# A graph layer on one core: the small fp32 products rewritten as rounded and remainder parts, the left-over rows stacked

## The reference, cut to what matters

```python
h = jnp.maximum(_layernorm(x, axis=-1), 0.0)            # x: 10000 x 128
hi = item_feat @ W_item.T + b_item                      # 10000 x 128
b  = h @ W_user.T + b_user
out = x + relu(adj @ hi + b)                            # adj: 10000 x 10000, f32
```

## Time and profile before

| | |
|---|---|
| median of 3 runs | 1114.21 us (1113.17 to 1114.88) |
| profiled execution, its own time | 1113.8 us |
| its span in the profile | 1112.0 us |
| TensorE busy | 1101.9 us (99%) |
| VectorE busy | 972.7 us (87%) |
| ScalarE busy | 768.1 us (69%) |
| TensorE's granted clock | 1.00 of full speed |
| moved by DMA | 421.50 MB, mean 379 GB/s |

### The profile page before, as it was taken

The page is one execution under the profiler, slowest core; times in us unless marked ns, Lnnn a source line. Parts: engine busy times, 40 slices in busy tenths (PEclk is TensorE's granted clock), DMA queues, the critical chain, the costliest instruction groups (busy, mean ns, idle before and its releaser), DMA issues.

```text
span 1112.0 us, 12241 instructions
## 1 busy us (share of the span) xinstructions
PE 1101.9 (99%) x5026; PEld 904.1 (81%) x5026; DVE 972.7 (87%) x692; ACT 768.1 (69%) x491; POOL 31.0 (3%) x62
## 2 busy tenths in 40 slices
PE   8999999999999999999999999999999999999998
PEld 7788788888888788888887888888788888888887
DVE  6999988889998888899998888999987889888887
ACT  5766766677776667776766677777766767776664
POOL 0000000001000000010000000000000000000000
PEclk9999999999999999999999999999999999999999
DMA  9999999999999999999999999999999999999994
GB/s 358 414 426 393 380 360 364 372 366 380 427 382 378 386 368 389 391 389 425 379 376 386 359 405 388 391 423 375 386 366 379 398 354 401 410 367 352 370 382 165
DMA packets 64904, 421.50 MB, mean 379 GB/s; under 512 B 7999, under 2 KB 8787, under 8 KB 25040
## 3 DMA queue, kind: packets, MB, share of 16 engines
q1 hardware_dynamic: 60128, 406.15, 93.1%
q0 software_dynamic: 4432, 14.44, 3.8%
q10 hardware_dynamic: 288, 0.13, 0.0%
HBM read 415.57 MB, written 5.12 MB: 378 GB/s over the span
## 4 chain that ended last, share of the span: by engine, by line
PE 91%; DVE 5%; DMA 1%; issue 1%; ACT 1%; SPq 0%; DVEq 0%; ACTq 0%
PE acc L578 29%; PE acc L571 29%; PE acc L572 29%; DVE lo_ring L379 4%; PE acc L544 2%; PE acc L521 1%; DMA a_ring<-in_adj_tiles 1%; ACT hi_ring L315 1%; DVE y L459 1%; PE acc L537 1%; PE acc L554 0%; DVE centred L422 0%; DVE stat L418 0%; SPq L219 0%; SPq L237 0%
## 5 line engine op out<-in xcount | busy, mean ns | idle before, releaser
L379 DVE TENSOR_TENSOR lo_ring<-a_ring,hi_ring 128x2048 fp32r<-128x2048 f32 (+1 forms) x387 | 861.5, 2239 | 120.3 <-ACT hi_ring L315 119.9
L315 ACT CAST hi_ring<-a_ring 128x2048 fp32r<-128x2048 f32 (+1 forms) x387 | 725.1, 1874 | 326.4 <-PE acc L578 321.6
L571 PE MATMUL acc<-hi_ring,h_lo 128*128 128x512 f32 (+1 forms) x1560 | 614.0, 394 | 1.2 <-ACT hi_ring L324 0.6
L578 PE MATMUL acc<-lo_ring,h_hi 128*128 128x512 f32 (+1 forms) x1560 | 603.0, 387 | 3.7 <-DVE lo_ring L379 3.7
L572 PE MATMUL acc<-hi_ring,h_hi 128*128 128x512 f32 (+1 forms) x1560 | 599.9, 385 | 0.0
L578 PEld LDWEIGHTS acc<-lo_ring,h_hi 128*128 128x128 f32 x1560 | 292.9, 188 | 68.1 <-DVE lo_ring L379 7.5
L571 PEld LDWEIGHTS acc<-hi_ring,h_lo 128*128 128x128 f32 x1560 | 293.1, 188 | 65.8 <-issue 9.1
L572 PEld LDWEIGHTS acc<-hi_ring,h_hi 128*128 128x128 f32 x1560 | 293.5, 188 | 61.9 <-issue 4.6
L521 PEld LDWEIGHTS acc<-wi,items 128*128 128x128 f32 x156 | 22.0, 196 | 2.0
L273 POOL DMA_DIRECT2D rows<-in_x_rows x20 | 10.9, 546 | 419.9 <-DVE centred L422 375.9
L521 PE MATMUL acc<-wi,items 128*128 128x128 f32 x156 | 22.2, 280 | 0.0
(11 more groups left out here) (31 smaller groups left out, 118.3 us busy)
## 6 DMA issues: line engine op xcount, KB each, us to landing
a_ring<-in_adj_tiles SPq DMA_DIRECT2D x311, 1024.0 KB, 7.1
a_ring<-in_adj_tiles SPq DMA_DIRECT2D x78, 904.0 KB, 6.6
rows<-in_x_rows POOLq DMA_DIRECT2D x19, 256.0 KB, 6.1
y<-in_x_t POOLq DMA_DIRECT2D x19, 256.0 KB, 7.1
items<-in_item_t SPq DMA_DIRECT2D x12, 384.0 KB, 7.7
out_t<-y POOLq DMA_DIRECT2D x16, 256.0 KB, 6.4
a_ring<-in_adj_tiles SPq DMA_DIRECT2D x4, 256.0 KB, 5.2
out_t<-y SPq DMA_DIRECT2D x3, 256.0 KB, 2.5
```

The lines of the kernel that those rows point to most:

```text
L315: nc.scalar.copy(hi_ring[:, r, 0:group_w(g)], a_ring[:, s, 0:group_w(g)]).then_inc(hi_written, 1)
L379: nc.vector.tensor_tensor(lo_ring[:, r, 0:n], a_ring[:, s, 0:n], hi_ring[:, r, 0:n], ALU.subtract).then_inc(lo_written[s], 1)
L571: nc.tensor.matmul(acc[k][:, 0:bank_w(g, k)], h_lo[:, c, :], hi, start=(c == 0), stop=False, skip_group_check=True)
L578: last = nc.tensor.matmul(acc[k][:, 0:bank_w(g, k)], h_hi[:, c, :], lo, start=False, stop=(c == CHUNKS - 1), skip_group_check=True)
```

## The change

The user product becomes three fp32r products: W_user is split once into `wu_hi` and `wu_lo`; ScalarE's copy out of PSUM now writes the rounded part `turned_hi`, and a new VectorE subtraction after tile 18 + 12k writes `turned_lo`. The products come before tile 20 + 12k instead of 18 + 12k.

The left-over product of a bank becomes one fp32r product over 50 rows. The moving side has the 16 adj rows three times (rounded, rounded, remainder) and two rows of ones; the weights are the rounded h, the remainder of h, the rounded h, and the rounded and remainder parts of b_user. Two banks stand side by side, at partitions 0 and 64, and the other two beside them in the free direction. SyncE loads 50 rows of 512 for each bank; at c = 38 ScalarE rounds 50 rows of 1024 twice and VectorE subtracts 16 rows of 1024 twice. `h_rem_product` moves from before tile 36 to before tile 10 of group 0, GpSimd moves six small pieces of the weights from SBUF to SBUF once, and `squares` and `normed` share a buffer. The descriptor scratch of the DMAs that GpSimd issues is set to 8192.

```diff
-ROWS_BLOCK = 32
+PAIR = 2
+ROWS_BLOCK = 64
+REM_ROWS = 3 * REM + 2
+REM_HI = 2 * REM
-H_REM_AT = 3 * BODY
-REM_AT = H_REM_AT + 4
+H_REM_AT = 10
+REM_AT = 3 * BODY + 4
+REM_ROUND_AT = REM_AT - 2
+WU_AT = 12
-USER_AT = 18
+USER_AT = 20
...
-                    sp.wait_ge(rem_used, g)
+                    sp.wait_ge(rem_lo_set, PAIR * g)
                 for k in range(ACC_BANKS):
-                    row = k * ROWS_BLOCK
-                    sp.dma_start(a_rem[row:row + REM, 0:bank_w(g, k)], adj_rem[g * ACC_BANKS + k, :, 0:bank_w(g, k)]).then_inc(rem_loaded, 16)
+                    row, n = k % PAIR * ROWS_BLOCK, BANK_W
+                    sp.dma_start(a_rem[row:row + REM_ROWS, k // PAIR, 0:n], adj_rem[g * ACC_BANKS + k, :, 0:n]).then_inc(rem_loaded, 16)
...
+            def move_rem_weights():
+
+                pool.wait_ge(h_rem_lo_set, 1)
+                pool.wait_ge(user_hi_set, 2)
+                pool.wait_ge(user_lo_set, 2)
+                for part in range(PAIR):
+                    row = part * ROWS_BLOCK
+                    pool.dma_start(h_rem[row + REM:row + 2 * REM, :], h_rem_lo[:, :]).then_inc(rem_moved, 16)
...
+            def left_over_round(g):
+                act.wait_ge(rem_loaded, (g + 1) * (16 * ACC_BANKS))
+                if g > 0:
+
+                    act.wait_ge(rem_used, g)
+                for part in range(PAIR):
+                    rows_p = slice(part * ROWS_BLOCK, part * ROWS_BLOCK + REM_ROWS)
+                    nc.scalar.copy(rem_parts[rows_p, :, :], a_rem[rows_p, :, :]).then_inc(rem_hi_set, 1)
...
-                act.wait_ge(turned_ready, g * UNITS + k + 1)
-                nc.scalar.copy(normed_t[:, 0:bank_w(g, k)], turned_of(g)[:, 0:bank_w(g, k)]).then_inc(normed_t_ready, 1)
+                u, n = g * UNITS + k, bank_w(g, k)
+                act.wait_ge(turned_ready, u + 1)
+                if u > 0:
+
+                    act.wait_ge(user_done, u)
+                nc.scalar.copy(turned_hi[:, 0:n], turned_of(g)[:, 0:n]).then_inc(turned_hi_set, 1)
...
+            def left_over_subtract(g):
+                for part in range(PAIR):
+                    rows_p = slice(part * ROWS_BLOCK + REM_HI, part * ROWS_BLOCK + REM_HI + REM)
+                    dve.wait_ge(rem_hi_set, g * PAIR + part + 1)
+                    nc.vector.tensor_tensor(rem_parts[rows_p, :, :], a_rem[rows_p, :, :], rem_parts[rows_p, :, :],
+                                            ALU.subtract).then_inc(rem_lo_set, 1)
+
+            def turned_subtract(g, k):
+                u, n = g * UNITS + k, bank_w(g, k)
+                dve.wait_ge(turned_hi_set, u + 1)
+                nc.vector.tensor_tensor(turned_lo[:, 0:n], turned_of(g)[:, 0:n], turned_hi[:, 0:n], ALU.subtract).then_inc(turned_lo_set, 1)
...
-                nc.tensor.matmul(acc_of(g)[k][:, 0:bank_w(g, k)], wu[:, :], normed_t[:, 0:bank_w(g, k)], start=False, stop=False,
-                                 skip_group_check=True)
+                nc.tensor.matmul(out[:, 0:n], wu_lo[:, :], turned_hi[:, 0:n], start=False, stop=False, skip_group_check=True)
+                nc.tensor.matmul(out[:, 0:n], wu_hi[:, :], turned_hi[:, 0:n], start=False, stop=False, skip_group_check=True)
+                pe.wait_ge(turned_lo_set, u + 1)
+                nc.tensor.matmul(out[:, 0:n], wu_hi[:, :], turned_lo[:, 0:n], start=False, stop=False,
+                                 skip_group_check=True).then_inc(user_done, 1)
...
-                pe.wait_ge(rem_loaded, (g + 1) * (16 * ACC_BANKS))
+                pe.wait_ge(rem_lo_set, PAIR * (g + 1))
                 for k in range(ACC_BANKS):
-                    rows_k = slice(k * ROWS_BLOCK, k * ROWS_BLOCK + REM + 1)
-                    last = nc.tensor.matmul(acc_of(g)[k][:, 0:bank_w(g, k)], h_rem[rows_k, :], a_rem[rows_k, 0:bank_w(g, k)],
+                    row, n = k % PAIR * ROWS_BLOCK, bank_w(g, k)
+                    rows_k = slice(row, row + REM_ROWS)
+                    last = nc.tensor.matmul(acc_of(g)[k][:, 0:n], h_rem[rows_k, :], rem_parts[rows_k, k // PAIR, 0:n],
                                             start=False, stop=False, skip_group_check=True)
```

More of the change, by code:

```diff
@@ L46 @@
 RING_GAP = 96
+DMA_SCRATCH = 8192
 CHUNKS = N_ITEM // P
@@ L78 @@
 assert PIECES * PIECE_TRIOS == TRIOS and PIECES == LOADS
-assert REM < ROWS_BLOCK and ACC_BANKS * ROWS_BLOCK <= P
+assert REM_ROWS <= ROWS_BLOCK and PAIR * ROWS_BLOCK <= P and ACC_BANKS % PAIR == 0
 F32 = mybir.dt.float32
@@ L170, in graph_layer @@
         rem_loaded = sem("rem_loaded")
-        ones_loaded = sem("ones_loaded")
+        rem_moved = sem("rem_moved")
+        rem_hi_set = sem("rem_hi_set")
+        rem_lo_set = sem("rem_lo_set")
+        h_rem_lo_set = sem("h_rem_lo_set")
+        user_hi_set = sem("user_hi_set")
+        user_lo_set = sem("user_lo_set")
         rows_loaded = sem("rows_loaded")
@@ L245, in _ @@
             sp.dma_start(wu[:, :], w_user_t).then_inc(user_loaded, 16)
[L246 to L249, removed]
+            sp.dma_start(bu[:, :], b_user).then_inc(user_loaded, 16)
             for g in range(GROUPS):
@@ L332, in h_rem_round, with user_round @@
                 act.wait_ge(h_rem_summed, 1)
-                for k in range(ACC_BANKS):
-                    row = k * ROWS_BLOCK
-                    nc.scalar.copy(h_rem[row:row + REM, :], h_full_rem[:, :]).then_inc(rem_set, 1)
+                for part in range(PAIR):
+                    for at in (0, REM_HI):
+                        row = part * ROWS_BLOCK + at
+                        nc.scalar.copy(h_rem[row:row + REM, :], h_full_rem[:, :]).then_inc(rem_set, 1)
+            def user_round():
+                act.wait_ge(user_loaded, 2 * 16)
+                nc.scalar.copy(wu_hi[:, :], wu[:, :]).then_inc(user_hi_set, 1)
+                nc.scalar.copy(bu_hi[:, :], bu[:, :]).then_inc(user_hi_set, 1)
+            def left_over_round(g):
[5 more added lines that the diff above has]
+                    nc.scalar.copy(rem_parts[rows_p, :, :], a_rem[rows_p, :, :]).then_inc(rem_hi_set, 1)
             def square(g, k):
@@ L363, in _ @@
                         h_round_hi(c // TRIO + 1)
-                    if g == 0 and c == REM_AT:
+                    if g == 0 and c == WU_AT:
+                        user_round()
+                    if g == 0 and c == H_REM_AT + 4:
                         h_rem_round()
+                    if c == REM_ROUND_AT:
+                        left_over_round(g)
                     for at, step in ((SQUARE_AT, square), (SQRT_AT, root_of_var), (COPY_AT, copy_turned)):
@@ L406, in h_rem_add_bias, with h_rem_subtract_lo, user_subtract_lo @@
                 nc.vector.tensor_tensor(h_full_rem[:, :], h_rem_bank[0:REM, 0:HID], bi[0:REM, :], ALU.add).then_inc(h_rem_summed, 1)
+            def h_rem_subtract_lo():
+                dve.wait_ge(rem_set, 1)
+                nc.vector.tensor_tensor(h_rem_lo[:, :], h_full_rem[:, :], h_rem[0:REM, :], ALU.subtract).then_inc(h_rem_lo_set, 1)
+            def user_subtract_lo():
+                dve.wait_ge(user_hi_set, 1)
+                nc.vector.tensor_tensor(wu_lo[:, :], wu[:, :], wu_hi[:, :], ALU.subtract).then_inc(user_lo_set, 1)
+                dve.wait_ge(user_hi_set, 2)
+                nc.vector.tensor_tensor(bu_lo[:, :], bu[:, :], bu_hi[:, :], ALU.subtract).then_inc(user_lo_set, 1)
+            def left_over_subtract(g):
+                for part in range(PAIR):
+                    rows_p = slice(part * ROWS_BLOCK + REM_HI, part * ROWS_BLOCK + REM_HI + REM)
[6 more added lines that the diff above has]
+                nc.vector.tensor_tensor(turned_lo[:, 0:n], turned_of(g)[:, 0:n], turned_hi[:, 0:n], ALU.subtract).then_inc(turned_lo_set, 1)
             steps = 6
@@ L494, in _ @@
                         empty(g - 1, 3)
-                    for at, step in ((CENTRE_AT, centre), (VAR_AT, variance), (NORM_AT, norm)):
+                    if c == REM_ROUND_AT:
+                        left_over_subtract(g)
+                    for at, step in ((CENTRE_AT, centre), (VAR_AT, variance), (NORM_AT, norm), (COPY_AT + 1, turned_subtract)):
                         k = unit_at(c, at)
@@ L633 @@
     left[:N_USER] = adj[:, full:]
+    left_rows = np.ones((GROUPS * ACC_BANKS, REM_ROWS, BANK_W), np.float32)
+    for part in range(3):
+        left_rows[:, part * REM:(part + 1) * REM] = left.reshape(GROUPS * ACC_BANKS, BANK_W, REM).transpose(0, 2, 1)
     x_rows = np.zeros((GROUPS * UNITS, ROW_T, ROW_TILES, HID), np.float32)
@@ L640 @@
         "adj_tiles": tiles.reshape(GROUPS, GROUP_W, CHUNKS, P).transpose(0, 2, 3, 1).reshape(GROUPS * CHUNKS, P, GROUP_W),
-        "adj_rem": left.reshape(GROUPS * ACC_BANKS, BANK_W, REM).transpose(0, 2, 1),
-        "ones_row": np.ones((1, BANK_W), np.float32),
+        "adj_rem": left_rows,
         "item_t": np.asarray(L0_gnn_item_feat).T,
```

49 lines of the change are left out of this document (36 added, 13 removed).

## The result

The changed kernel takes 1115.92 us (median of 20 runs, 1114.5 to 1118.16), the kernel before 1114.28 (20 runs). The ratio is 1.0015, with a 95% interval of 1.0008 to 1.0021: slower by 0.15%, less than the 0.2% set as the bound, and clear of zero. The forecast was 1111.8 with a range of 1109.0 to 1114.2; the time lies outside it. The profiled execution has a span of 1114.3 us, 2.3 more than before.

A forecast was written before the change was run, and what follows sets the result against it. TensorE was taken to bound the kernel, driving a ring, if later stages keep up. 3.8 + 2.1 - 2.1 - 0.6 - 0.1 - 0.6 = 2.5 us off 1113.8 gave 1111.3, median 1111.8, range 1109.0 to 1114.2.

The forecast's parts named there:

- User product: TensorE's user product: three fp32r products cost 0.68 us against 0.88 for fp32, saving 0.20 a unit, 3.8 us in all.
- Left-over products: TensorE's left-over products of a group: 0.84 us instead of 1.27, saving 0.43 a group, 2.1 us in five.
- no toll: Rival: the 0.39 us for switching from 128 rows to blocks and back vanishes with fp32r; 1110.2 us, chance 0.14.
- pairs don't run side by side: Rival: TensorE's two pairs of 50-row left-over products run one after another, costing 1.30 us; 1113.5 us, chance 0.15.
- VectorE's left-over subtractions: Two subtractions after tile 38 make TensorE wait 0.5 us at tile 39, 41 in group 0: -2.1 and -0.6 us.
- 1.22 at 1024 and 1.13 back to back; the pair is 2.26: VectorE's 1024-wide left-over subtraction: time in us set by width, alone, in a row, and for two.
- margin of 1.80: Tile 39, group 1: 1.80 us from the end of VectorE's subtraction to bank 0's third product on TensorE.
- no VectorE stall: Rival: the left-over subtractions cost 1.2 us or are taken up, so TensorE does not wait; 1109.1 us, chance 0.08.
- The loads: Four left-over loads ahead of tile 12 grow from 32 to 100 KB: 0.2 to 0.3 us in group 0, -0.6 total.
- Delays of 0.65 to 1.2 us: How much later tiles behind the larger left-over loads land, by bytes at 425 GB/s or by fewer DMA engines.
- the slow rival: 50-row loads make tile 12 3.6 us late, costing 12 us over five groups, 1123 us; chance 0.08 with other slow cases.
- The moved h_rem_product: The product L527, moved before tile 10 of group 0, costs the same there, perhaps 0.1 us more: -0.1.

The follow-up runs named there:

- user part alone: Kernel before with only the user product split into three fp32r products before tile 20 + 12k, left-over part untouched: 1111.23 us, ratio 0.9976.
- casts_early: Changed kernel with ScalarE's two left-over casts after tile 34 instead of 38, VectorE's subtractions still after 38: 1115.79 us, ratio 1.0020.
- rows48: Changed kernel with left-over loads of 48 rows instead of 50, the two rows of ones loaded once at the start: 1116.26 us, ratio 1.0019.
- not in place: Changed kernel with the first left-over subtraction of a group writing to its own tile, not over its input, and descriptor scratch 4096: one profiled run, 1115.98 us.
- late loads: Changed kernel with the four 50-row left-over loads of a group issued ahead of tile 24 instead of tile 12: 1114.13 us, ratio 1.0000.

## Why the prediction was wrong

It had the mechanisms and nearly all their places, and mis-sized three terms, all to the same side: measured 1115.9 against 1111.8. The three are 1.3, 2.5 and 1.2 us off, 5.0 together where the forecast is off by 4.1; two of them are read from medians and one from the ledger of one profile, so they need not add up.

- **User product, 3.8 forecast.** The user part alone gained 2.5 us by the medians (0.24% by the ratio); in its profile 0.9 came from elsewhere. The step that failed is "three fp32r products cost 0.68": in this place they cost 0.72, and some products behind them come 0.235 apart instead of 0.227, so a unit gave 0.13 (0.08 in group 0), not 0.20. That VectorE's new subtraction is hidden was right.
- **Left-over products, 2.1 forecast.** Right: 0.87 against 1.27, 2.0 in five groups, with the toll that the prediction kept. By the rule of the Trainium skill, "TensorEngine Tiling (Array Packing)", section Key Properties (a change of mode drains TensorE), the trace agrees: L647 starts 0.32 us after the product before it, where L554 started 0.31 after, so the late start stands in blocks of 64 rows as of 32, with fp32r as with fp32. That the late start is a drain, the trace alone doesn't show. The rivals "no toll" and "pairs don't run side by side" fall.
- **VectorE's left-over subtractions, -2.1 and -0.6 forecast.** Forecast at half its size, at the right tiles but for one: 0.96 us in group 1 instead of 0.5, 1.0 a group in five, 5.2 us where 2.7 stood. In group 0 the wait was forecast at tile 41 alone and fell on 39 and 41, at 0.5 each. The step that failed is "1.22 at 1024 and 1.13 back to back; the pair is 2.26". The 1.22 was exact (mean 1219 ns). But the overlap of 0.09 with the neighbours, which "back to back" took for granted, is missing at all three seams and a gap of 0.03 stands there, which makes 0.12 a seam, so the pair takes 2.62; and TensorE's restart costs 0.11 more. Since the margin of 1.80 is subtracted from the whole, 0.36 us more of burst and 0.11 of restart doubled the wait. The rival "no VectorE stall" falls; `casts_early` shows that ScalarE's casts were hidden, as argued.
- **The loads, -0.6 forecast.** They cost 1.8 us by the median, 1.9 in group 0 of this profile. The step that failed is "Delays of 0.65 to 1.2 us": tile 12 landed 15.3 us after its issue where it had 12.5, 2.8 later. That is later than the 2.2 from which the slow rival was to decide, and one of the prediction's signs of being wrong (ScalarE's wait for loads grows by several us: 4.3 to 8.5) came true. But the rival's price was wrong too: it had all five groups pay, and in this profile only group 0 did, as the tiles of group 1 came 0.5 to 1.7 later and still in time. The Trainium skill, "DMA: Bandwidth & Descriptors", section Why a DMA increments its semaphore by 16 and not by 1, would have 50 rows on 10 engines and 48 rows on 16; the 128 packets more of `rows48` agree with that, and its median shows no gain from it.
- **The moved h_rem_product, -0.1 forecast.** +0.05 by the ledger: right.

The account of the profile closes: 2.0 us gained with the left-over products and 3.0 with the user products (by the ledger: 1.6 in groups 1 to 3, 1.1 in group 4, 0.3 in group 0), 5.2 lost to VectorE's bursts, 1.9 to the loads, 0.4 at the start. That is 2.5, where the ledger ends at 2.4; the medians are 1.6 apart. VectorE's busy time grew by 21, not by 26; ScalarE's by 10, as forecast.

## What to carry to other kernels

Small work moved from the bounding engine to a helper that keeps up with little room is paid by where it stands, not by its sum: 2.5 us of VectorE work behind another burst cost 1.0 us a group, and the same work in two halves in a quiet stretch cost nothing. Read the margin tile by tile before placing it, and price seams as well as durations. Look too at what a small load is queued ahead of: 400 KB in front of the tile that already arrives just in time cost 1.8 us, and nothing two rounds of the ring later.

## What the runs showed of the hardware that was not expected

VectorE's instructions in a row, when the second waits for nothing that the first does, mostly overlap by 0.07 to 0.09 us in these traces. The left-over subtractions, which start at partition 32, 64 or 96, have a gap of 0.03 us in front of them and behind them instead, in every group, as large as between the small `stat` subtractions of which each waits for the result of the one before. A 16-partition subtraction that starts at partition 0 overlaps with the one before it. All of these seams fit a rule by which the overlap is lost where the start partition changes; no run parts that from other rules.

TensorE's 512-wide products have two paces, 0.227 and about 0.235 us, at a granted clock of 1.0. The slower one follows an interruption, such as a wait, a user product or a product of another shape, and lasts for several products. In group 4 it can last for whole tiles: there a tile takes 2.42 or 2.47 us, and the user part alone ran its last tiles at 2.42 where the kernel before had 2.47, 0.9 us in all. So did the profiles of "casts early" and "not in place", while those of the changed kernel and of late loads stayed at 2.47. What sets it was not found.
